# Gathering chunks in a graph layer on one Trainium2 core: from 128-row products on whole windows to 32-row products on four lanes

## The reference

```python
h_self   = x @ W_lin + b_lin                          # x: 12500 nodes x 128
messages = x[dst] @ W_msg + b_msg                     # 200000 edges (src, dst), sorted by dst
msg_sum  = segment_sum(messages, src, 12500)
counts   = segment_sum(ones, src, 12500)
h_agg    = msg_sum / max(counts, 1)
h        = relu(concat([h_self, h_agg], 1) @ W_upd + b_upd)
out      = layernorm(x + h)                           # over the 128 features, eps 1e-5
```

## Time and profile before

| | |
|---|---|
| median of 3 runs | 1325.19 us (1324.97 to 1325.33) |
| profiled execution, span of its instructions | 1375.4 us |
| granted clock, mean | 0.957 |
| busy: PE, PEld, DVE, ACT, POOL | 1203.5, 715.2, 997.9, 710.7, 498.1 us |
| second part begins at about | 425 us |

### The profile page before, as it was taken

How to read it: one execution, slowest core, us unless ns; L and a number is a source line. 1 busy time by engine, 2 the same in 40 slices (tenths; PEclk the granted TensorE clock), 3 DMA queues, 4 the chain that set the end, 5 groups by cost and what they waited for, 6 DMA issues and landing times. The chain is left out here.

```text
span 1375.4 us, 41041 instructions
## 1 busy us (share of the span) xinstructions
PE 1203.5 (88%) x15996; PEld 715.2 (52%) x15996; DVE 997.9 (73%) x2543; ACT 710.7 (52%) x1027; POOL 498.1 (36%) x503
## 2 busy tenths in 40 slices
PE   1949899887884799999999999999999999999996
PEld 1948798876871344444444444444444444444443
DVE  7999999999995266666666666666666666666665
ACT  0313333310111476666666766666666666666664
POOL 3000000000004555555455555555555555555540
PEclk9979999998876799999999999999999999999998
DMA  7213233213407244444444444444444344444420
GB/s 103 97 47 102 97 111 106 77 45 104 111 5 231 66 123 129 124 137 137 135 137 139 135 138 138 137 137 137 122 125 117 120 120 132 136 137 138 138 62 12
DMA packets 120430, 156.27 MB, mean 114 GB/s; under 512 B 32314, under 2 KB 90279, under 8 KB 120166
## 3 DMA queue, kind: packets, MB, share of 16 engines
q1 hardware_dynamic: 95932, 105.62, 24.3%
q0 software_dynamic: 23024, 47.31, 13.8%
q10 hardware_dynamic: 1290, 0.74, 0.2%
HBM read 130.46 MB, written 23.17 MB: 112 GB/s over the span
## 5 line engine op out<-in xcount | busy, mean ns | idle before, releaser
L610 ACT ACTIVATE big<-slot 128x768 bf16<-128x768 f32 x800 | 608.2, 809 | 332.2 <-PE slot L1326 305.7
L1326 PE MATMUL slot<-big 128*128 128x384 bf16 x2600 | 498.4, 328 | 45.0 <-ACT big L610 38.2
L675 POOL DMA_INDIRECT big<-x,dst_at x400 | 407.0, 1018 | 335.8 <-PE slot L1326 153.6
L989 DVE TENSOR_SCALAR big<-big,iota_k 128x512 bf16<-128x512 f16 x650 | 220.5, 371 | 332.9 <-PE slot L1326 305.0
L1326 PEld LDWEIGHTS slot<-big 128*128 128x128 bf16 x2600 | 216.0, 97 | 305.8 <-issue 126.8
L1340 PE MATMUL acc<-big 32*128 32x385 bf16 x6400 | 335.7, 325 | 9.4 <-issue 9.3
L1340 PEld LDWEIGHTS acc<-big 32*128 32x128 bf16 x6400 | 133.4, 93 | 184.7 <-issue 123.6
L999 DVE TENSOR_TENSOR big<-col_lo,iota_lo 128x512 bf16<-128x512 f16 x400 | 166.3, 416 | 0.0
L669 POOL MEMSET big<- 128x4 bf16 x6 | 0.3, 96 | 412.4 <-issue 412.4
L1240 PE MATMUL acc<-big 125*100 125x64 f16 x1600 | 85.3, 215 | 25.8 <-DVE big L877 25.7
L679 POOL DMA_INDIRECT big<-x,sp_i x75 | 76.9, 1026 | 84.6 <-PE acc L1363 40.1
(11 more groups left out here) (150 smaller groups left out, 810.9 us busy)
## 6 DMA issues: line engine op xcount, KB each, us to landing
big<-rows SPq DMA_DIRECT2D x25, 2048.0 KB
big<-in_x SPq DMA_DIRECT2D x48, 256.0 KB, 3.3
x<-big SPq DMA_DIRECT2D x24, 384.0 KB, 2.6
big<-x,dst_at POOLq DMA_INDIRECT x400
base<-big SPq DMA_DIRECT2D x24, 256.0 KB, 2.5
big<-x SPq DMA_DIRECT2D x32, 192.0 KB, 2.4
big<-base SPq DMA_DIRECT2D x24, 256.0 KB
out<-big SPq DMA_DIRECT2D x24, 256.0 KB
```

The source lines that it names most:

```text
L610: act.activation(xg[n % NX][:, :, 0:F3], slot[n % 2][:, :, 0:F3], ACT.Copy).then_inc(s["xg_ready"], 1)
L675: pool.indirect_dma_start(out=xg_d[:, c, 0:F3], out_offset=None, in_=x3_dram, in_offset=bass.IndirectOffsetOnAxis(ap=dst_at[:, q, c:c + 1] ...
L989: last = nc.vector.tensor_scalar(W[R_ % NW_][:, k, :].rearrange("p (c h n) -> p c h n", c=4, h=4), brow[q % NB].rearrange("p (h c n) -> p ...
L1326: ins = nc.tensor.matmul(slot[n % 2][:, j, 0:F3], W[R_ % NW_][:, k, (c % 4) * P:(c % 4 + 1) * P], xwin[:, win_at(c) + k, :], start=k == 0, ...
```

## The change

The gathering of the first 64 chunks is put on four lanes. The chunk 4g + i belongs to lane i, which is the SBUF partitions 32i to 32i + 31. A window is held as pieces of 32 nodes: `n_win(c)` says how many (1 to 9, by a line fitted to the chunk's number), and piece k of chunk 4g + i lies in `xwin[32i:32i+32, WIN_AT[g] + k]`. The distances of a lane are on its own 32 partitions of `brow`. A gathering product has 32 rows, and lane i accumulates in its own bank, `slot[i // 2][:, i % 2]`; there is one bank a lane. ACT evicts each bank by itself, 384 columns, and each lane has its own semaphore `gathered[i]`. `W` holds the one-hots of a whole quad, 83 of 128 columns, in two copies; they are made by nine instructions, one for each piece number k over all runs that have it. `L` is made for two runs with one signal; L and xg have four copies.

`take_sums` is cut in two halves of two banks. POOL's `PACE` is gone; it waits only until the place it writes is free. The runs are in the order 8, 0, 9, 1, ... 15, 7, and pairs and spills are added at other runs. TensorE's sequence is no longer a loop: `lane_of` describes one lane's products, with the time from which each may start in steps of one product (`APART`, `TAKEN`, `FREED`), and a merge writes the four lanes into one order, at each point the product that may start first. Adding of a run comes two runs after its gathering. Window loads are 64 of at most 9 x 32 rows, and all are issued before the first `brow`.

```diff
+    RUNS = CP // 4
+    def n_win(c):
+        return math.ceil((4.356 * c + 5.35) / SL) if c < CP else 12
+    RUN_WIN = [n_win(4 * g + 3) for g in range(RUNS)]
+    NK = max(RUN_WIN)
+    WIN_AT = [sum(RUN_WIN[:g]) for g in range(RUNS + 1)]
+    NWIN = WIN_AT[RUNS]
+    FIRST_RUN = [min(g for g in range(RUNS) if RUN_WIN[g] > k) for k in range(NK)]
+    HOT_AT = [sum(RUNS - f for f in FIRST_RUN[:k]) for k in range(NK)]
+    assert RUN_WIN == sorted(RUN_WIN) and all(n_win(4 * g) > 0 for g in range(RUNS))
+    def hot_at(g, k):
+        return HOT_AT[k] + g - FIRST_RUN[k]
...
-    NWIN = win_at(CP - 1) + n_win(CP - 1)
-    NWIN_A = win_at(60)
...
-    rows_dram = nc.dram_tensor("rows", [H, C, SL], f16, kind="Internal").ap()
+    rows_dram = nc.dram_tensor("rows", [H, 4, RUNS, SL], f16, kind="Internal").ap()
...
-        NB, NW_, NL, NX, ND = 2, 4, 6, 6, CD // 2
+        NB, NW_, NL, NX, ND = 2, 2, 4, 4, CD // 2
-        brow = [two.take(CP * P, f16) for _ in range(NB)]
-        W = [shaped(two.take(3 * 4 * P, bf16), "p (k n) -> p k n", k=3) for _ in range(NW_)]
-        L = [shaped(two.take(4 * P, bf16), "p (a n j) -> p a n j", a=2, j=2) for _ in range(NL)]
+        W = [shaped(two.take(NWIN * P, bf16), "p (w n) -> p w n", n=P) for _ in range(NW_)]
+        brow = [shaped(two.take(RUNS * P, f16), "p (h g n) -> p g h n", h=4, n=SL) for _ in range(NB)]
+        L = [shaped(two.take(8 * P, bf16), "p (b a n j) -> p b a n j", b=2, a=2, j=2) for _ in range(NL)]
...
-        xg = [shaped(two.take(2 * FG, bf16), "p (c f) -> p c f", f=FG) for _ in range(NX)]
+        xg = [shaped(two.take(4 * FG, bf16), "p (c f) -> p c f", f=FG) for _ in range(NX)]
...
-        ORDER = [7, 0, 8, 1, 9, 2, 10, 3, 15, 4, 11, 5, 12, 6, 13, 14]
-        assert sorted(ORDER) == list(range(RUNS))
-        STEPS = 2 * RUNS
+        ORDER = [g for a in range(RUNS // 2) for g in (a + RUNS // 2, a)]
         LAYER, ROOT, NORM = 7, 8, 9
-        PAIR_RUNS, SPILL_RUNS = [3, 4, 6, 7, 9, 10, 12, 14], [2, 5, 8, 11, 13, 15]
+        def l_of(R, i):
+            return L[R // 2 % NL][:, R % 2, i // 2, :, i % 2]
+        FIRST_ADD = 3
+        PAIR_RUNS, SPILL_RUNS = [4, 6, 8, 10, 11, 13, 15, 17], [5, 7, 9, 12, 14, 16]
...
+            def load_window(c):
+                g, lane, n = c // 4, c % 4, n_win(c)
+                low = sp.value_load(low_i[0:1, c:c + 1], min_val=0, max_val=N - 1)
+                sp.dma_start(xwin[lane * SL:(lane + 1) * SL, WIN_AT[g]:WIN_AT[g] + n, :],
+                             x3_dram[bass.ds(low, n * SL), :].rearrange("(k p) f -> p k f", p=SL)).then_inc(s["wins_loaded"], 16)
+            for c in range(CP):
+                load_window(c)
...
-                if q >= 2:
-                    sp.wait_ge(s["W_ready"], (q - 1) * RUNS)
-                rows = rows_dram[q * 4:q * 4 + 4, 0:CP, :].rearrange("h c n -> h (c n)").unsqueeze(0).to_broadcast([P, 4, CP * SL])
-                sp.dma_start(brow[q % NB].rearrange("p (h e) -> p h e", h=4), rows).then_inc(brow_loaded[q % NB], 16)
+                if q >= NB:
+                    sp.wait_ge(s["W_ready"], q - NB + 1)
+                for lane in range(4):
+                    rows = rows_dram[q * 4:q * 4 + 4, lane, :, :].rearrange("h g n -> h (g n)").unsqueeze(0).to_broadcast([SL, 4, RUNS * SL])
+                    sp.dma_start(brow[q % NB][lane * SL:(lane + 1) * SL, :, :, :].rearrange("p g h n -> p h (g n)"), rows).then_inc(brow_loaded[q % NB], 16)
...
-                def take_rows(n):
-                    act.wait_ge(s["gathered"], n + 1)
-                    if n >= NX:
-                        act.wait_ge(s["aggregated"], n - NX + 1)
-                    act.activation(xg[n % NX][:, :, 0:F3], slot[n % 2][:, :, 0:F3], ACT.Copy).then_inc(s["xg_ready"], 1)
+                def take_rows(R, i):
+                    act.wait_ge(gathered[i], R + 1)
+                    if R >= NX and i == 0:
+                        act.wait_ge(s["aggregated"], R - NX + 1)
+                    act.activation(xg[R % NX][:, i, 0:F3], slot[i // 2][:, i % 2, 0:F3], ACT.Copy).then_inc(s["xg_ready"], 1)
...
-                        if q == 0 and i == len(GATHERS) // 2:
+                        if q == 0 and i == RARE_AFTER:
...
-                        _, name, steps = PACE[i]
-                        if (q - 1) * PER_QUAD[name] + steps > 0:
-                            pool.wait_ge(s[name], (q - 1) * PER_QUAD[name] + steps)
...
+                def hot_windows(q, k):
+                    if k == 0:
+                        dve.wait_ge(brow_loaded[q % NB], 64 * (q // NB + 1))
+                        if q >= NW_:
+                            for lane in range(4):
+                                dve.wait_ge(gathered[lane], RUNS * (q - NW_ + 1))
+                    f = FIRST_RUN[k]
+                    ins = nc.vector.tensor_scalar(W[q % NW_][:, HOT_AT[k]:HOT_AT[k] + RUNS - f, :].rearrange("p g (h n) -> p g h n", n=SL),
+                                                  brow[q % NB][:, f:RUNS, :, :], iota_k[:, k:k + 1], None, ALU.is_equal)
+                    if k == NK - 1:
+                        ins.then_inc(s["W_ready"], 1)
+                def hot_nodes(P_):
+                    q, a = P_ // (RUNS // 2), P_ % (RUNS // 2)
+                    if P_ >= NL:
+                        dve.wait_ge(s["aggregated"], 2 * (P_ - NL + 1))
+                    for b in range(2):
+                        g = ORDER[2 * a + b]
+                        cols = col_lo[:, q, g * 4:g * 4 + 4].rearrange("p (a j) -> p a j", j=2)
+                        ins = nc.vector.tensor_tensor(L[P_ % NL][:, b, :, :, :], spread2(cols, P), tbl(iota_lo[:, :, :], 2), ALU.is_equal)
+                    ins.then_inc(s["L_ready"], 1)
...
+                    if half == 0:
+                        dve.wait_ge(s["half_added"], q + 1)
+                    else:
+                        dve.wait_ge(s["aggregated"], (q + 1) * RUNS)
                     if q > 0:
                         dve.wait_ge(s["S_read"], q)
-                    nc.vector.tensor_scalar(cnt[:, 0, :], accs[:, :, F3], 1.0, None, ALU.max).then_inc(s["counts_taken"], 1)
-                    nc.vector.tensor_scalar(cnt[:, 2, :], accs[:, :, F3], 1.0, None, ALU.min)
-                    nc.vector.tensor_reduce(S, accs[:, :, 0:F3].rearrange("p h (k f) -> p h f k", k=3), AX.X, ALU.add).then_inc(s["sums_taken"], 1)
...
-                def gather(q, t):
-                    n = q * STEPS + t
-                    R_ = n // 2
-                    pe.wait_ge(s["W_ready"], R_ + 1)
-                    if n == 2 * ORDER.index(15):
-                        pe.wait_ge(s["tail_wins_loaded"], 16 * (CP - 60))
-                    if n >= 2:
-                        pe.wait_ge(s["xg_ready"], n - 1)
-                    for j in range(2):
-                        c = ORDER[t // 2] * 4 + t % 2 * 2 + j
-                        for k in range(n_win(c)):
-                            ins = nc.tensor.matmul(slot[n % 2][:, j, 0:F3], W[R_ % NW_][:, k, (c % 4) * P:(c % 4 + 1) * P], xwin[:, win_at(c) + k, :],
-                                                   start=k == 0, stop=k == n_win(c) - 1)
-                    ins.then_inc(s["gathered"], 1)
...
+                APART, TAKEN, FREED = 2.4, 5.1, 14.0
+                def gather_step(R, lane, k):
+                    q, g = R // RUNS, ORDER[R % RUNS]
+                    c = 4 * g + lane
+                    if k == 0 and R % RUNS == 0 and lane == 0:
+                        pe.wait_ge(s["W_ready"], q + 1)
+                    if k == 0 and R > 0:
+                        pe.wait_ge(s["xg_ready"], 4 * (R - 1) + lane + 1)
+                    rows, last = slice(lane * SL, (lane + 1) * SL), k == n_win(c) - 1
+                    ins = nc.tensor.matmul(slot[lane // 2][:, lane % 2, 0:F3], W[q % NW_][rows, hot_at(g, k), :], xwin[rows, WIN_AT[g] + k, :],
+                                           start=k == 0, stop=last)
+                    if last:
+                        ins.then_inc(gathered[lane], 1)
+                def add_step(R, lane, i):
+                    q, r = divmod(R, RUNS)
+                    if i == 0:
+                        pe.wait_ge(s["xg_ready"], 4 * R + 4)
+                        pe.wait_ge(s["L_ready"], R // 2 + 1)
+                        if r == 0 and q > 0:
+                            pe.wait_ge(s["sums_taken"], 2 * (q - 1) + lane // 2 + 1)
+                    rows, last = slice(lane * SL, (lane + 1) * SL), i == 3
+                    ins = nc.tensor.matmul(acc[lane][:, 0:F3 + 1], l_of(R, i)[rows, :], xg[R % NX][rows, i, 0:F3 + 1],
+                                           start=r == 0 and i == 0, stop=last and r == RUNS - 1)
+                    if last and lane == 3:
+                        ins.then_inc(s["aggregated"], 1)
+                    elif last and lane == 1 and r == RUNS - 1:
+                        ins.then_inc(s["half_added"], 1)
...
+                    for R in range(NR + 2):
+                        if R < NR:
```

(18 more changed lines are left out.)

323 lines of the change are left out of this document (131 added, 192 removed).

## The result

The changed kernel takes **1267.1 us** (median of 4 runs, 1265.2 to 1286.5) against 1325.1 us before: ratio 0.956, 95% interval 0.9547 to 0.9573. The highest of the four, 1.7% above the lowest, is a slow run and not in the ratio. The kernel is 58 us faster, where 145 were forecast, and lies 5 us above the forecast range.

What follows compares the result with a forecast made beforehand. TensorE was taken to set the pace. A quad: 28.1 + 1.5 + 0.5 + 0.3 = 30.4 us in place of 36.4, so 25 save 150 us; with +5 at the start, 1325.2 becomes 1180 us, range 1135 to 1262.

Steps and rivals of the forecast that it cites:

- One quad lasts 36.4 us: Kernel before, second part: time of one quad from the profiled count instructions, (1364.0 - 489.8) / 24, the base of the saving.
- rival D: More is won: start's standstill goes (20 us) and a quad takes 29.4 us, 1135 us in all; chance 0.08.
- All of it lies beside other work: nothing: Gathers, window loads and row copies: hidden beside other work, cost 0; uncovered, one late gather holds PE up to 1 us.
- TensorE's work: Per quad, 661 products of 32 rows make 165.25 steps, 27.0 us, the floor if four lanes always work.
- the lane's chain: One PSUM bank a lane: pieces plus eviction holes filled with adding products, 171.8 steps or 28.1 us on lane 3.
- ACT's pace: 64 evictions a quad, four in a run 1.54 us: small runs filled up to 9.4 steps, 1.5 us a quad.
- the root: ACT's root waits for DVE's `layer` behind three large one-hots: bounds 0 to 1 us a quad, taken as 0.
- Double waits: 120 places with two waits a quad on TensorE, 7 to 25 ns each, 0.8 to 3.0 us; taken as 0.5 us.
- +5 us: Start: all nine one-hots of the quad must stand before PE begins, 6 us, so PE starts 5 us later.
- A, evictions: ACT's evictions never overlap and bound the kernel: 31.7 us a quad, 1213 us in all; chance 0.14.
- B, double waits at full price: 120 double waits at 25 ns each, 3.0 us: 32.9 us a quad, 1243 us in all; chance 0.13.
- C, lanes in step: Lanes wait together and evictions follow in a row: 45 us a quad, 1545 us, slower; chance 0.08.

Runs made afterwards that it cites:

- e1: The kernel from before the change, unchanged, profiled once more: 1323.49 us.
- e7: Changed kernel with row copies a quad early and one a run, and the loads of x and base made to wait for later runs: 1210.6 us.
- e5: Changed kernel with the row copies dropped after the first two quads, 512 KB less a quad: 1218.2 us.
- e11: e7 with each wait of TensorE asked only if it has not yet asked that semaphore for as much: 1199.4 us.
- e8: e7 with ACT evicting 96 columns in place of 384 from the fifth run on: 1186.8 us.
- e17: Changed kernel with row copies in 4 KB pieces of other data, the 32 partitions in one dimension (sixteen DMA engines): 1274.0 us.
- e16: Changed kernel with row copies in 4 KB pieces of other data, the 32 partitions given as 4 x 8 (four DMA engines): 1226.6 us.
- e4: Changed kernel with the row copies issued one quad earlier, a little later after the loads: 1237.8 us.

## Why the prediction was wrong

**The sign and the mechanism of the gain held; its size did not.** Forecast 145 us, measured 58. The 87 us between split by the two quads: 25 x (36.4 - 35.2) = 30 us are before's, 25 x (32.8 - 30.4) = 60 us are the changed kernel's, and the start gives 3 back.

- **"One quad lasts 36.4 us"** failed as a base. It came from one execution 50 us over the median, and in e1 a quad took 35.2. The text subtracted the gain of that execution from the median of the others, though its own sum of rows came to 35.7 (some 34.8 with the 0.65 us of waits for ACT that e1 shows). The same execution had the standstill (rival D's 20 us), which e1 has not.
- **"All of it lies beside other work: nothing", on gathers and loads.** This is the step that cost most. The DMA share of 0.43 was right (0.42 now), and no load was late for its reader, but the transfers held up TensorE's instructions. e7 moves only transfers and gives back 25 x (32.8 - 30.6) = 55 us (56.5 between the medians). The sentence bounded a late gather at "up to 1 us"; the holes were up to 4.1 us, with a clock of 0.60 behind.
- **TensorE's work**, 661 products in steps of 0.1635 us, and the lane's chain, 28.1 us: the parts that could be read were borne out. Products took 0.326 and 0.328 us with those after holes in, 0.322 in e5; the eviction 0.496 (forecast 0.49); 7925 gathering products (forecast some 7,900). e7's quad of 30.6, and 29.9 with single waits (e11: (1187.1 - 1.0 - 468.9) / 24), stand beside the sum of 30.4. That the sum comes so near is in part luck, since the terms below were off in both directions; no run shows the 28.1 us, or the 0.3 us of the quad's end, by itself.
- **ACT's pace, 1.5 us, and the root, put at 0.** PE waited for ACT 17.5 us in 23 quads, 0.8 a quad, not "2 to 3", and nearly all of that is not the evictions' pace. From 480 to 1180 us, 22 of its 24 such waits, one a quad, end 0.73 us after the start of ACT's root (L571), which itself had waited for DVE's `mv`, 26.1 us in 23 of the 25 quads:

```profile
709.56 0.30 ACT L571 ACTIVATE std<-mv,eps 128x4 f32<-128x4 f32 x1 [0.80 <-DVE mv L1016]
...
710.29 0.33 PE L1286 MATMUL slot<-big 32*128 32x384 bf16 x1 [0.70 <-ACT big L567]
```

  So the wait behind the root, which the text put at nothing ("I take 0, as `layer` comes three runs after the step that lets DVE on"), costs about 0.7 us a quad. e8 halved the eviction and took 0.95 us off, less than the 1.5 to 2.5 expected; PE's waits for ACT stayed (15.7 us, 14.1 in e7), so what it gained is not idle time of PE, and that it is the pace of the small runs is only argued.
- **Double waits, 0.5 us.** e11: at most 0.45, for 114 waits a quad, so 4 ns each at most and not 7 to 25.
- **DVE.** Nine one-hots took 155.1 us in 25 quads, 6.2 each (6 forecast), and 6.04 us at the start, where PE began at 429.75 in place of 426.27 (425.63 in e1). Of the "+5 us" for it PE's start shows 3.5 to 4.1, and none is left by the first sum, which stands at 465.6 us in both e1 and the changed kernel, and between 465.6 and 470.0 in the variants.
- **Changes of tile shape, 3.1 us a quad.** The Trainium skill, "TensorEngine Tiling (Array Packing)", Key Properties, says that a switch of the mode drains TensorE; the rows agree with 0.10 us a switch, and no run here tests them alone.
- **The rivals.** A, evictions (1213 us): not so; by e8 they are worth 24 us with half their length taken away, and ACT was idle 124 us. The rule of the Trainium skill, "TensorEngine Tiling (Array Packing)", PSUM Bottleneck, that the copy out of PSUM may become the bottleneck, holds here only in part. B, double waits at full price (1243): it named the nearest time, and with 32.9 us the right quad, for a wrong reason; its 3.0 us a quad were at most 0.45. C, lanes in step (1545): no sign of it; 661 x 0.1635 / 32.8 = 3.3 lanes at work, 3.5 in e7, where it needed less than 2.97. D (1135): its standstill is in neither e1 nor the changed kernel, and no quad came to 29.4 us with all the work in it.

**What stays open.** That the burst's transfers make the holes is shown by moving, dropping and reshaping them; that it goes through the instruction packets rests on the late packet of q8 before each of the 14 holes over 1.5 us, and on the same in e17: 19 such holes, each over 2.4 to 3.0 us after a packet's start. e7 and e16 have none. No run changed the instruction packets and nothing else. Where such a packet waits before it starts, no row tells, nor why fewer engines help. Why e4's small shift gives 29 us was not taken further, and no run moves ACT's root.

## What to carry to other kernels

When an edit makes TensorE's products smaller and denser, its instruction stream becomes a load of its own: look at the "issue" idle time of PE and at the packets of the instruction queue, and count the transfers that are issued together, not only their share of the DMA. If PE shows holes with no releaser behind a burst, spread the burst over the loop, or shape its copies so that they take fewer DMA engines; both are free where the data has a quad to arrive. And take the base of a forecast from an execution whose time is that of the median: here a second profile of the old kernel would have mended a third of the miss (30 of 87 us).
